# A third chunk normalised among the experts, and an end shared out between three engines, in a one-core mixture-of-experts kernel

## The chip, the cores and the metric

The kernel runs on one core of a Trainium2 chip. The metric is the device time of that core in microseconds (us). Engines: TensorE (PE, and PEld for its weight loads), VectorE (DVE), ScalarE (ACT), GpSimd (POOL), and SyncE (SP), which issues most DMAs. Each takes its instructions in order; semaphores join them.

## The reference, cut to what matters

The input x is 16 batches of 128 rows of 128 numbers, 2048 rows in all. Four blocks are added to it in turn. The change touches the seam inside the first block and the end of the last one.

```python
x = x + L0_attn(L0_cond(x))   # L0_cond: shared expert + two chosen experts of 8 (gelu(g) * u @ down)
                              # L0_attn: layer norm; u, v, base = silu(xn @ W); quadratic attention; @ Wo
x = x + L0_ffn(L0_cond2(x))   # quantised feed-forward, scales from maxima over the whole tensor
x = x + L1_attn(L1_cond(x))
x = x + L1_ffn(L1_cond2(x))   # L1_ffn, the last:
    w = router weights (rows x 16)
    q, k, v = einsum('ne,neh->nh', w, x @ proj[e])      # for each of three projections
    o = softmax(q k^T / sqrt(128)) v
    out = einsum('enh,ehc->nc', w[:, e] * o, o_proj)    # 16 experts e
```

## The kernel before, in words

The rows stand in four chunks `c` of 512 rows (columns of the transposed tiles), each of four tiles `b` of 128. A product that needs more than half precision is written as three f16 matmuls (high by high, and the two mixed ones: `PASSES`, `SPLIT`); an f32 matmul of 128x128 shows as two records.

**The experts of the first block.** The list `order` (L226 to L235) fixes the order of the units on TensorE, ScalarE and VectorE by hand: 16 shared units, then four groups of eight expert units ("ex"). A unit is `up` on TensorE into a pair of PSUM banks (`pair(k)`, three pairs in turn), gelu on ScalarE (L905), the gating product on VectorE (L1366), a half-precision copy on ScalarE (L915), its rest on VectorE (L1372), and three places later `down` on TensorE. Between the units stand steps of the layer norm of chunks already finished: "mean" (L450, then `centred`, L1303, and ScalarE's square), "var" (L455, `variance`), and "rs": ScalarE writes the inverse root as a diagonal (`diag`, L884, four activations of 128x128), TensorE spreads it (`rstd`, L464), VectorE scales (`xg`, L1337), ScalarE and VectorE split the result in two halves (`xn_hi` L893, `xn_lo` L1341). The inverse root itself is a chain of small VectorE instructions on 128xn numbers (`inverse_root`, L1311 to L1332), each waiting for the one before.

In the kernel before, chunks 0 and 1 are wholly normalised among the experts of group 3. Chunk 2 has mean and variance there. Chunk 3 has nothing, since its rows are ready only with the last unit (L1397). What is left stands behind the experts: TensorE L479 to L521, ScalarE L928 to L951, VectorE L1406 to L1423. There are three projections `base`, `u0`, `u1` of each chunk (L496), each followed by a silu on ScalarE (L935); chunk c uses bank BK[4 + c] for all three, so each waits for the silu before it. After them come a small product for the third block (`ret_amm`, copied by ScalarE at L951), eight steps of `v` (L538, L542, silu L961), VectorE's quantisation of feed-forward weights (`prep_fw`, L1251), 32 rotations (L1436) whose inputs GpSimd prepares (L1858), and `fw_lo` (L1428), which waits for ScalarE's copies of the turned weights (L973). VectorE's next work (L1445 on) comes behind `fw_lo`.

**The end.** For chunks 0 to 2, `output(n)` on TensorE multiplies a tile of attention output by four experts' matrices (three f16 matmuls of 128x512, L809) into one of three banks. VectorE's `gather(n)` (L1751) adds the four blocks into the tile of XT, each times its column of router weights: four dependent instructions. There are 48 such groups, four for each tile, and `RW` (the weights) is multiplied by the softmax's inverse sums beforehand (L1799). The third bank turn of `output` waits for a gather three groups back.

Chunk 3 goes another way. When its attention output is in BK[4] (`attend(3, 2)`, L796, which waits for ScalarE's `ptt(3)`, L1103), VectorE weighs it for each of the 16 experts (`ZW[e1]`, L1817), and TensorE multiplies each by the expert's matrix in f32, 128x128 for each tile (`weighed_output`, L841), summing in four banks. Experts 12 to 15 are done tile by tile, and each tile is finished by one instruction of VectorE (L1825). The gathers of the last four groups of chunk 2, 44 to 47 (they are tile 11), stand between the weighings. SyncE sends each tile of 64 KB out as it is finished (L1993), in the order of the tiles.

Of the kernel before, what the change touches and what calls it, by code (L numbers as in the profile page):

```python
# [13 lines left out]
ALU = mybir.AluOpType  # L14
# [37 lines left out]
    (("down", 48), ("weffmm", 4), ("ret_amm", 1), ("fwt", 3), ("wbotmm", 8), ("zmm", 4), ("mlp_down", 16), ("prod_o", 48), ("tile", 4)),  # L52
# [12 lines left out]
     ("ff_max", 24), ("gate16", 4), ("gated_ff", 5), ("ot_ff", 4), ("o_lo", 12), ("x2", 4), ("pp", 4), ("w2", 2), ("weighed", 64), ("zw", 16)),  # L65
# [4 lines left out]
    (("x_lo", 4), ("xq", 4), ("quant", 12), ("ot_lo", 3)),  # L70
    (("route", 30), ("router", 114), ("rw", 3), ("done", 4)),
# [41 lines left out]
def program(nc, A, out):  # L113
    with ExitStack() as ctx:
# [112 lines left out]
        for g in range(4):  # L227
            ex = [("ex", 4 * g + bi, s) for bi in range(4) for s in range(2)]
            if g:
                ex[6:6] = [("var", g - 1, 0)]  # L230
                ex[4:4] = [("mean", g - 1, 0)]
            if g == 3:
                ex[3:3] = [("rs", 1, 0)]
                ex[2:2] = [("rs", 0, 0)]
            order += ex  # L235
# [27 lines left out]
        ROOT = 12  # L263
# [23 lines left out]
        BK_M = [BK[i] for i in (7, 2, 3, 1, 0, 1, 0, 1)]  # L287
        PROJ = {"base": (512, "bb", BASE), "u0": (0, "bu0", U0), "u1": (128, "bu1", U1)}
# [86 lines left out]
        ZW += [STG[:, i // 3, 512 * (i % 3):512 * (i % 3) + 512] for i in range(6)] + [PK0T[:, 512 * i:512 * i + 512] for i in range(2)]  # L375
        SPREADS = 4
# [8 lines left out]
        def tensor(e):  # L385
# [101 lines left out]
            def project(name, c):  # L487
# [4 lines left out]
                else:  # L492
                    q.wait_ge({"u0": "base", "u1": "u0"}[name], c + 1)
                w = PROJ[name][0]
                for n, (wp, xp) in enumerate(SPLIT):
                    t = e.matmul(BK[4 + c][:, :], AW16[:, wp, w:w + 128], XH[:, xp, cc(c)], start=(n == 0), stop=(n == 2))  # L496
                t.then_inc(S(name + "mm"), 1)

            q.wait_ge("gated", UNITS)
            weff(0)  # L500
# [4 lines left out]
            project("base", 1)  # L505
            weff(2)
            weff(3)
            project("u0", 0)
            project("u0", 1)
            q.wait_ge("cent", 4)  # L510
            rstd(2, BK[0])
            q.wait_ge("var", 4)
            rstd(3, BK[1])
            for c in range(2):
                project("u1", c)
            for name in ("base", "u0", "u1"):
                for c in (2, 3):
                    project(name, c)
# [4 lines left out]
            def turn_ffn(i):  # L523
                q.wait_ge("prep", PREP["fq"])
                q.wait_ge("u1", i + 1)
# [310 lines left out]
            def weighed_output(e1, b):  # L836
# [4 lines left out]
                return e.matmul(BK_T[b][:, 0:128], ZW[e1][:, bb_(b)], WO[:, bb_(e1)], start=(e1 == 0), stop=(e1 == 15), skip_group_check=True)  # L841
# [11 lines left out]
        def scalar(e):  # L853
# [30 lines left out]
            def diag(c):  # L884
                q.wait_ge("root", ROOT if c < 2 else 2 * ROOT)
# [9 lines left out]
            for k in range(NU + 3):  # L895
                if k + 1 < NU and order[k + 1][0] == "rs":
                    diag(order[k + 1][1])
                if k < NU and order[k - 1][0] == "rs":
# [33 lines left out]
            def project(name, c):  # L932
                _, b, dst = PROJ[name]
                q.wait_ge(name + "mm", c + 1)
                e.activation(dst[:, cc(c)], BK[4 + c][:, :], ACT.Silu, bias=col(b), scale=1.0 / AS).then_inc(S(name), 1)  # L935

            project("base", 0)
            project("base", 1)
            diag(2)
            diag(3)  # L940
            project("u0", 0)
            xn_hi(2)
            project("u0", 1)
            xn_hi(3)
            for c in range(2):
                project("u1", c)
            for name in ("base", "u0", "u1"):
                for c in (2, 3):
                    project(name, c)
# [155 lines left out]
            for k in range(STEPS):  # L1105
# [22 lines left out]
                if k >= LAG and k < NI + LAG and (k - LAG) % 16 == 15:  # L1128
# [4 lines left out]
                    e.activation(VS[:, cc(c)], BK[2][:, :], ACT.Copy).then_inc(S("qv_out"), 1)  # L1133
            softmax(3)
            ptt(3)

        def vector(e):
# [167 lines left out]
            def variance(c, bank):  # L1305
                q.wait_ge("varmm", c + 1)
                if c == 2:
                    e.tensor_copy(sm(15), bank[:, 16:32]).then_inc(S("sim_sq"), 1)
# [776 lines left out]
```

## Time and profile before

| what | us |
|---|---|
| median of 3 runs | 487.17 (486.77 to 487.62) |
| profiled execution, its own time | 487.26 |
| its span, first to last instruction | 485.5 |
| TensorE busy | 435.0 (90%) |
| VectorE busy | 411.2 (85%) |
| ScalarE busy | 244.7 (50%) |
| GpSimd busy | 63.3 (13%) |

The span runs from the first to the last instruction; 1.76 us of the profiled execution lie around it. All times below are counted from the span's start. Busy shares are averages over stages with different limits. In the timelines each row is an instruction or a run of equal ones: start, duration, engine, line, operation, output and inputs with shapes, and in brackets how long the engine had been idle before it and for whom. Durations of one engine overlap a little, so the step from one start to the next is shorter than a duration.

### The profile page before, as it was taken

How to read it: one execution, taken by the hardware profiler on the slowest of the kernel's cores; microseconds unless marked ns; L12 is line 12 of the kernel's file. 1: busy time of each engine (PE TensorE's matmuls, PEld its weight loads, DVE VectorE, ACT ScalarE, POOL GpSimd, SP SyncE). 2: the span in 40 equal slices, each digit the busy share in tenths (PEclk: the TensorE clock that was granted, in tenths of full speed). 3: DMA queues.
4: the chain of work that ended last, by engine and by line, in shares of the span. 5: the costliest groups of instructions: out<-in, count | busy, mean ns of one | idle time of the engine just before them, and what ended most of it. 6: DMA issues, size and time to landing. Idle time of an engine off the chain costs nothing.

```text
span 485.5 us, 9701 instructions
## 1 busy us (share of the span) xinstructions
PE 435.0 (90%) x3783; PEld 302.5 (62%) x3783; DVE 411.2 (85%) x919; ACT 244.7 (50%) x446; POOL 63.3 (13%) x77
## 2 busy tenths in 40 slices
PE   8999999998898989202999999999999999999997
PEld 6447998987357654000389867667666555655576
DVE  6997889786698769999866789986998999989786
ACT  5976554474767549893666463336224222422110
POOL 0007000000690706300090000000000000000000
PEclk9999999999999999755899999999999999999999
DMA  8979996960560005303330025637753000000000
GB/s 274 355 304 395 388 383 280 372 269 10 166 174 1 1 0 159 101 14 124 122 99 1 1 76 189 212 139 248 259 195 97 7 12 7 5 7 7 5 7 28
DMA packets 24629, 66.71 MB, mean 137 GB/s; under 512 B 3108, under 2 KB 6567, under 8 KB 24455
## 3 DMA queue, kind: packets, MB, share of 16 engines
q1 hardware_dynamic: 24144, 65.98, 37.7%
q8 instruction: 30, 0.49, 0.4%
q10 hardware_dynamic: 438, 0.11, 0.1%
q14 instruction: 17, 0.13, 0.1%
HBM read 38.68 MB, written 1.18 MB: 82 GB/s over the span
## 4 chain that ended last, share of the span: by engine, by line
PE 29%; DVE 22%; issue 4%; ACT 1%; DVEq 0%; ACTq 0%
PE bk L764 10%; DVE XT L1751 6%; PE bk L772 5%; DVE X L1739 3%; PE bk L809 3%; DVE RA L1779 3%; PE bk L631 2%; DVE RA L1558 1%; DVE WK L1600 1%; PE bk L784 1%; PE bk L674 1%; PE bk L640 1%; PE bk L691 1%; DVE QS L1466 1%; PE bk L700 1%
## 5 line engine op out<-in xcount | busy, mean ns | idle before, releaser
L764 PE MATMUL bk<-X,RB 128*128 128x512 f16 x384 | 94.6, 383 | 0.7 <-DVE X L1739 0.4
L1069 ACT ACTIVATE X<-RA 128x512 f16<-128x512 f32 x64 | 40.3, 630 | 101.2 <-DVE RA L1779 83.9
L1751 DVE SCALAR_TENSOR_TENSOR XT<-bk,WK,XT 128x128 f32<-128x128 f32 x192 | 67.0, 349 | 5.4 <-issue 0.2
L764 PEld LDWEIGHTS bk<-X,RB 128*128 128x128 f16 x384 | 37.1, 99 | 42.3 <-DVE X L1739 1.6
L772 PEld LDWEIGHTS bk<-RB,X 128*128 128x128 f16 x768 | 48.8, 99 | 15.4 <-issue 0.6
L772 PE MATMUL bk<-RB,X 128*128 128x128 f16 x768 | 53.8, 220 | 0.0
L1739 DVE TENSOR_TENSOR X<-RA,X 128x512 f16<-128x512 f32 x64 | 43.9, 685 | 1.3 <-ACT X L1069 1.3
L905 ACT ACTIVATE WK<-bk 128x512 f32<-128x512 f32 x48 | 28.6, 595 | 27.5 <-PE bk L418 21.7
L809 PE MATMUL bk<-RB,RA 128*128 128x512 f16 x144 | 38.8, 379 | 0.9 <-DVE RA L1796 0.9
L1366 DVE SCALAR_TENSOR_TENSOR RB<-WK,WCOL,bk 128x512 f32<-128x512 f32 x32 | 23.7, 744 | 10.1 <-ACT WK L905 10.1
L418 PE MATMUL bk<-X,RC 128*128 128x128 f16 x480 | 29.7, 219 | 0.0
L1372 DVE TENSOR_TENSOR RB<-RB 128x512 f16<-128x512 f32 x36 | 25.6, 712 | 3.9 <-ACT RB L915 3.6
L418 PEld LDWEIGHTS bk<-X,RC 128*128 128x128 f16 x480 | 27.9, 98 | 0.9
L915 ACT ACTIVATE RB<-RB 128x512 f16<-128x512 f32 x36 | 22.4, 624 | 5.8 <-DVE RB L1366 5.6
L413 PE MATMUL bk<-X,STG 128*128 128x512 f16 x96 | 22.8, 379 | 0.2 <-DVE X L1179 0.2
L1466 DVE TENSOR_REDUCE QS<-RA 128x1 f32<-128x512 f32 (+2 forms) x28 | 22.4, 837 | 0.1
L594 PE MATMUL bk<-PK1T,QS 128*128 128x128 f32 x5 | 2.1, 413 | 20.5 <-DVE QS L1469 20.5
L1858 POOL TENSOR_SCALAR RA<-RA,ROPE 128x128 f32<-128x128 f32 x16 | 9.4, 590 | 81.4 <-ACT RA L935 81.4
L413 PEld LDWEIGHTS bk<-X,STG 128*128 128x128 f16 x96 | 9.3, 97 | 15.5 <-issue 6.0
L447 PE MATMUL bk<-RB,RC 128*128 128x128 f16 x240 | 16.6, 219 | 2.6 <-DVE RB L1372 2.6
L809 PEld LDWEIGHTS bk<-RB,RA 128*128 128x128 f16 x144 | 12.7, 98 | 7.3 <-DVE RA L1796 1.3
L447 PEld LDWEIGHTS bk<-RB,RC 128*128 128x128 f16 x240 | 14.2, 98 | 4.7 <-DVE RB L1372 2.9
(345 smaller groups left out, 884.9 us busy)
## 6 DMA issues: line engine op xcount, KB each, us to landing
RC<-RA SPq DMA_DIRECT2D x20, 768.0 KB, 5.2
STG<-RA SPq DMA_DIRECT2D x8, 768.0 KB, 5.4
RC<-expert_weights SPq DMA_DIRECT2D x22, 256.0 KB, 6.0
RC<-in_wx SPq DMA_DIRECT2D x7, 768.0 KB, 7.8
X<-in_w SPq DMA_DIRECT2D x8, 512.0 KB, 3.5
RA<-RA SPq DMA_DIRECT2D x4, 768.0 KB, 5.1
STG<-expert_weights SPq DMA_DIRECT2D x12, 256.0 KB, 5.9
QT<-expert_weights SPq DMA_DIRECT2D x8, 256.0 KB, 5.0
```

What stands on the lines that cost most here:

```text
L413: t = e.matmul(bank[:, :], W16[:, o:o + 128], X16[:, xp, cc(a)], start=(n == 0), stop=(n == 2))
L418: t = e.matmul(bank[:, bb_(jj)], w[:, o:o + 128], X16[:, xp, bb_(a)], start=(n == 0), stop=(n == 2))
L447: t = e.matmul(bank[:, bb_(a % 4)], w[:, o:o + 128], H16[:, u % 3, xp, bb_(jj)], start=(j == 0 and jj == 0 and n == 0), stop=(j == 1 and j ...
L764: t = e.matmul(BK[m][:, :], P16[:, wp, wo:wo + 128], ZH[:, n % 4, xp, :], start=(e1 == 0 and i == 0), stop=(e1 == 15 and i == 2))
L772: t = e.matmul(BK[2][:, bb_(b)], ZH[:, n % 4, xp, bb_(b)], P16[:, wp, wo:wo + 128], start=(e1 == 0 and b == 0 and i == 0), stop=(e1 == 15 ...
L809: t = e.matmul(bank_o(n)[:, :], OT16[:, xp, bb_(4 * c + b)], P16[:, wp, 6144 + 512 * g:6656 + 512 * g], start=(i == 0), stop=(i == 2))
L905: e.activation(ge[u % 3], pair(k)[0][:, :], ACT.Gelu_apprx_tanh, scale=1.0 / WS).then_inc(S("gelu"), 1)
L1069: e.activation(ZH[:, r, 0, :], zf[r], ACT.Copy).then_inc(S("z_hi"), 1)
L1372: tt(H16[:, u % 3, 1, :], hf[u % 3], H16[:, u % 3, 0, :], ALU.subtract).then_inc(S("h_lo"), 1)
L1466: return red(dst, src, X_AX, ALU.max, apply_absolute_value=True)
L1739: tt(ZH[:, n % 4, 1, :], zf[n % 4], ZH[:, n % 4, 0, :], ALU.subtract).then_inc(S("zlo"), 1)
L1751: stt(XT[:, bb_(t_)], bank_o(n)[:, bb_(i)], RW[:, t_, e1:e1 + 1], XT[:, bb_(t_)], ALU.mult, ALU.add).then_inc(S("acc"), 1)
```

## The change

1. `order` of group 3 holds mean 2 one place earlier and a new last place, "rs" of chunk 2. The root of chunk 2 is a chain of its own, ten steps, spread over the places behind "var" 2. `ROOT` is 10: the clamp below is dropped for the layer norm and moved into another instruction for the router's columns, and the clamp above is done once for those columns alone, behind the last chain.
2. Behind the experts only chunk 3 is normalised. The projections run over chunks 0, 1, 2 first and chunk 3 last; in chunk 3 `u0` uses bank 6 instead of 7. `prep_fw(0)` is moved up, before `xg(3)`.
3. At the end the gathers of groups 44 to 47 leave VectorE. ScalarE (`late`) multiplies the four blocks of each by their weights into SBUF, and GpSimd adds the sixteen blocks together (six additions) and to the tile.
4. Chunk 3 is weighed before the product for experts 0 to 11 (`PRE` = 12). Experts 12 to 15 are weighed behind it: TensorE does four more `output` groups, 48 to 51, and VectorE four more gathers. This needs the attention output of chunk 3 in halves (two instructions of VectorE from BK[4]) and `RW` of chunk 3 times its inverse sums (one small one).

```diff
+                ex = ex[0:2] + [("rs", 0, 0), ex[2], ("rs", 1, 0), ("mean", 2, 0)] + ex[3:5] + [("var", 2, 0)] + ex[5:8] + [("rs", 2, 0)]
-        ROOT = 12
+        ROOT = 10
+        def bank_p(name, c):
+            return BK[6 if c == 3 and name == "u0" else 4 + c]
+        PRE, LATE = 12, 44
+        groups += [(3, b, 3) for b in range(4)]
+        WGT = [XF[:, 512 * i:512 * i + 512] for i in range(4)]
@@ TensorE behind the experts @@
             q.wait_ge("gated", UNITS)
+            q.wait_ge("xg", 3)
...
             project("base", 1)
+            project("base", 2)
             weff(2)
             weff(3)
-            project("u0", 0)
-            project("u0", 1)
-            q.wait_ge("cent", 4)
-            rstd(2, BK[0])
+            for c in range(3):
+                project("u0", c)
             q.wait_ge("var", 4)
             rstd(3, BK[1])
-            for c in range(2):
+            for c in range(3):
                 project("u1", c)
             for name in ("base", "u0", "u1"):
-                for c in (2, 3):
-                    project(name, c)
+                project(name, 3)
@@ project(u0, 3) waits for u1 of chunk 2, project(u1, 3) for base of chunk 3 @@
@@ output(n) @@
-                q.wait_ge(*(("acc", 4 * (n - 2)) if n >= 3 else ("wts", 3)))
+                if n < 3:
+                    q.wait_ge("wts", 3)
+                elif LATE <= n - 3 < LATE + 4:
+                    q.wait_ge("late_w", n - 2 - LATE)
+                else:
+                    q.wait_ge("acc", 4 * (n - 2 if n - 3 < LATE else n - 6))
...
-            for e1 in range(12):
+            for e1 in range(PRE - 2):
                 for b in range(4):
                     weighed_output(e1, b)
-                if e1 in (0, 4):
-                    output(46 + (e1 == 4))
+                if e1 in (0, 1, 3, 5, 7, 9):
+                    output({0: 46, 1: 47, 3: 48, 5: 49, 7: 50, 9: 51}[e1])
             for b in range(4):
-                for e1 in range(12, 16):
+                for e1 in range(PRE - 2, PRE):
                     t = weighed_output(e1, b)
@@ ScalarE behind the experts @@
-            project("base", 0)
-            project("base", 1)
-            diag(2)
+            for c in range(3):
+                project("base", c)
             diag(3)
-            project("u0", 0)
-            xn_hi(2)
-            project("u0", 1)
+            for c in range(2):
+                project("u0", c)
             xn_hi(3)
-            for c in range(2):
+            project("u0", 2)
+            for c in range(3):
                 project("u1", c)
             for name in ("base", "u0", "u1"):
-                for c in (2, 3):
-                    project(name, c)
+                project(name, 3)
@@ ScalarE at the end @@
+            def late(n):
+                q.wait_ge("prod_o", n + 1)
+                for i in range(4):
+                    e1 = 4 * g + i
+                    t = e.activation(WGT[n - LATE][:, bb_(i)], bank_o(n)[:, bb_(i)], ACT.Copy, scale=RW[:, t_, e1:e1 + 1])
             softmax(3)
+            late(44)
             ptt(3)
+            for n in range(45, 48):
+                late(n)
@@ VectorE behind the experts @@
-            for _ in inverse_root(8, 32):
+            for _ in inverse_root(12, 32):
                 pass
+            then(root)
+            ts(SNS, SNS, 1e12, None, ALU.min)
             weff(2)
-            xg(2, BK[0])
+            prep_fw(0)
             xg(3, BK[1])
+            xn_lo(3)
             weff(3)
-            xn_lo(2)
-            xn_lo(3)
@@ VectorE at the end @@
-            for e1 in range(16):
+            tt(RW[:, 12:16, :], RW[:, 12:16, :], RS[:, 12:16] (broadcast), ALU.mult)
+            for e1 in range(PRE):
                 tt(ZW[e1], BK[4][:, :], WR[16 + e1], ALU.mult)
-                if e1 in (1, 4, 7, 10):
-                    gather({1: 44, 4: 45, 7: 46, 10: 47}[e1])
+                if e1 == 2:
+                    e.tensor_copy(OT16[:, 0, cc(3)], BK[4][:, :])
+                    tt(OT16[:, 1, cc(3)], BK[4][:, :], OT16[:, 0, cc(3)], ALU.subtract)
+                if e1 in (6, 8, 10, 11):
+                    gather({6: 48, 8: 49, 10: 50, 11: 51}[e1])
@@ GpSimd at the end: SUM = WGT[0]; plus WGT[1], WGT[2], WGT[3] (128x512 each), then its halves @@
@@ (128x256, 128x128), then XT of tile 11 plus SUM (128x128), "summed"; tile 11 is sent on "summed" @@
```

## Rows read from the trace of the kernel before

**Rows 1.** The page: busy time, share and instructions by engine.
```profile
PE 435.0 (90%) x3783; PEld 302.5 (62%) x3783; DVE 411.2 (85%) x919; ACT 244.7 (50%) x446; POOL 63.3 (13%) x77
```

**Rows 2.** The chain that ended last, in order of time, 452 us on: start, us.
```profile
462.61 0.65 PE bk L809 x3
463.25 0.04 issue
463.29 1.17 PE bk L796 x8
...
464.49 1.29 DVE RA L1817 x2
...
483.07 0.35 DVE XT L1825
```

**Rows 3.** Timeline of VectorE behind the experts.
```profile
119.75 0.69 DVE L1397 SCALAR_TENSOR_TENSOR QT<-bk,QT 128x512 f32<-128x512 f32 x1 [0.94 <-PE bk L447]
...
124.35 0.18 DVE L1314 TENSOR_SCALAR SM<-SM 128x24 f32<-128x24 f32 x1
124.56 0.18 DVE L1317 TENSOR_SCALAR SM<-SM 128x24 int32<-128x24 int32 x1
...
129.51 0.75 DVE L1337 SCALAR_TENSOR_TENSOR QT<-QT,COL,bk 128x512 f32<-128x512 f32 x1 [2.00 <-PE bk L466]
130.67 0.75 DVE L1337 SCALAR_TENSOR_TENSOR QT<-QT,COL,bk 128x512 f32<-128x512 f32 x1 [0.42 <-PE bk L466]
...
133.38 1.34 DVE L1254 TENSOR_REDUCE QS<-RB 128x36 f32<-128x1152 f32 x1
...
150.76 1.49 DVE L1428 SCALAR_TENSOR_TENSOR FW<-bk,FW 128x384 f16<-128x384 f32 x3 [1.55 <-ACT FW L973]
```

**Rows 4.** Timeline of ScalarE behind the experts.
```profile
126.95 2.44 ACT L888 ACTIVATE WK<-PK1T,SM 128x128 f32<-128x128 f32 x8 [1.27 <-DVE SM L1330]
...
132.10 1.25 ACT L935 ACTIVATE RA<-bk,COL 128x512 f32<-128x512 f32 x2
...
138.08 0.27 ACT L951 ACTIVATE ATT<-bk 128x128 f32<-128x128 f32 x1
```

**Rows 5.** Timeline of TensorE at the last experts and behind them.
```profile
118.09 1.63 PE L447 MATMUL bk<-RB,RC 128*128 128x128 f16 x24 [1.41 <-DVE RB L1372]
...
124.62 1.88 PE L485 MATMUL bk<-WEFF,PK0T 128*128 128x512 f32 x4
126.34 1.46 PE L496 MATMUL bk<-WBOT,AW 128*128 128x512 f16 x6
128.37 2.26 PE L466 MATMUL bk<-WK,ONES 128*128 128x512 f32 x4 [0.57 <-ACT WK L888]
...
132.74 4.72 PE L496 MATMUL bk<-WBOT,AW 128*128 128x512 f16 x18 [0.28 <-DVE WBOT L1341]
137.29 0.38 PE L521 MATMUL bk<-ATT,PK2T 128*128 128x128 f32 x2
138.49 0.37 PE L538 MATMUL bk<-BVD,ON 3*128 3x512 bf16 x1 [0.82 <-ACT ATT L951]
```

**Rows 6.** Timeline of ScalarE: the last softmax, and four activations of PSUM in a row.
```profile
462.01 0.21 ACT L1098 ACTIVATION_READ_ACCUMULATOR WK<-bk,SM 128x1 f32 x1
462.64 0.60 ACT L1103 ACTIVATE RA<-bk 128x512 f32<-128x512 f32 x1 [0.42 <-PE bk L790]
```
```profile
264.13 1.21 ACT L1045 ACTIVATE WK<-bk,BSEL 128x128 f32<-128x128 f32 x4
```

**Rows 7.** Timeline of VectorE at the end.
```profile
465.69 1.50 DVE L1751 SCALAR_TENSOR_TENSOR XT<-bk,WK,XT 128x128 f32<-128x128 f32 x4
467.11 1.28 DVE L1817 TENSOR_TENSOR RA<-bk,WBOT 128x512 f32<-128x512 f32 x2
```

**Rows 8.** Timeline of TensorE at the end: two matmuls of f32 to a row.
```profile
480.19 0.61 PE L841 MATMUL bk<-WEFF,STG 128*128 128x128 f32 x4
480.64 0.61 PE L841 MATMUL bk<-WEFF,PK0T 128*128 128x128 f32 x4
```

**Rows 9.** One line each: durations in ns, min/median/max, first and last start.
```profile
L1404 DVE TENSOR_TENSOR WEFF<-bk,PK0T x4: 679/682/684, 122.3 to 131.3; 128x512 f32<-128x512 f32 x4
```
```profile
L1858 POOL TENSOR_SCALAR RA<-RA,ROPE x16: 447/452/1648, 125.3 to 144.7; 128x128 f32<-128x128 f32 x16
```
```profile
L1835 POOL TENSOR_TENSOR RB<-RB x1: 2810/2810/2810, 37.8 to 37.8; 128x1024 f32<-128x1024 f32 x1
```
```profile
L1993 SPq DMA_DIRECT2D out<-XT x16: 332/332/433, 369.4 to 483.4; - x16
```

More of the change, by code:

```diff
@@ L897, in scalar @@
                     diag(order[k + 1][1])
-                if k < NU and order[k - 1][0] == "rs":
+                if 0 < k <= NU and order[k - 1][0] == "rs":
                     xn_hi(order[k - 1][1])
@@ L1313, in inverse_root @@
                 v, y, h = SMF[:, 224 + a:224 + b], SMF[:, 544 + a:544 + b], SMF[:, 256 + a:256 + b]
-                ts(v, v, 1e-30, None, ALU.max).then_inc(root.next(), 1)
-                yield
-                then(root)
+                if root.n:
+                    then(root)
                 ts(y.bitcast(I32), v.bitcast(I32), -0.5, 1597463007.0, ALU.mult, ALU.add).then_inc(root.next(), 1)
@@ L1328, in inverse_root @@
                     yield
-                then(root)
-                ts(y, y, 1e12, None, ALU.min).then_inc(root.next(), 1)
                 assert root.n % ROOT == 0
-                yield
             def xg(c, bank):
@@ L1388, in vector @@
                     next(first_half, None)
-                if k - 2 < NU and order[k - 2][0] == "rs":
+                if 2 <= k < NU + 2 and order[k - 2][0] == "rs":
                     xn_lo(order[k - 2][1])
@@ L1411, in vector @@
             q.wait_ge("sim_sq", 1)
-            for _ in inverse_root(8, 32):
+            for _ in inverse_root(12, 32):
                 pass
+            then(root)
+            ts(SNS, SNS, 1e12, None, ALU.min).then_inc(root.next(), 1)
             weff(2)
-            xg(2, BK[0])
+            prep_fw(0)
             xg(3, BK[1])
+            xn_lo(3)
             weff(3)
-            xn_lo(2)
-            xn_lo(3)
             then(root)
             tt(SNT, pk1("sim"), SNS, ALU.mult).then_inc(S("sn"), 1)
-            for part in range(4):
+            for part in range(1, 4):
                 prep_fw(part)
@@ L1743, in gather @@
                 t_ = 4 * c + b
+                first = n if n < LATE else n - 4
                 q.wait_ge("prod_o", n + 1)
@@ L1877, in gpsimd @@
                 e.tensor_tensor(lo, src, hi, ALU.subtract).then_inc(S("p16"), 1)
+            SUM = WGT[0]
+            for g in range(1, 4):
+                q.wait_ge("late_w", g + 1)
+                if g > 1:
+                    q.wait_ge("sum", g - 1)
+                e.tensor_tensor(SUM, SUM, WGT[g], ALU.add).then_inc(S("sum"), 1)
+            q.wait_ge("sum", 3)
+            e.tensor_tensor(SUM[:, 0:256], SUM[:, 0:256], SUM[:, 256:512], ALU.add).then_inc(S("sum"), 1)
+            q.wait_ge("sum", 4)
+            e.tensor_tensor(SUM[:, 0:128], SUM[:, 0:128], SUM[:, 128:256], ALU.add).then_inc(S("sum"), 1)
+            q.wait_ge("sum", 5)
+            q.wait_ge("turned", 3)
+            e.tensor_tensor(XT[:, bb_(11)], XT[:, bb_(11)], SUM[:, 0:128], ALU.add).then_inc(S("summed"), 1)
         def sync(e):
@@ L1991, in sync @@
                     t_ = 4 * c + b
-                    q.wait_ge(*(("acc", 4 * groups.index((c, b, 3)) + 4) if c < 3 else ("done", b + 1)))
+                    q.wait_ge(*(("done", b + 1) if c == 3 else ("summed", 1) if t_ == 11 else ("acc", 4 * groups.index((c, b, 3)) + 4)))
                     e.dma_start(out[bb_(t_), :], XT[:, bb_(t_)]).then_inc(S(f"out{c}"), 16)
```

47 lines of the change are left out of this document (29 added, 18 removed).

## The prediction, made before the change was run

> **What bounds the kernel now.** I read the page first: TensorE 90% busy, VectorE 85% [rows 1]. No single engine is the bound, so what matters is which wait ends last at the two places the change touches. The chain that ended last was the second view. It answers for the end of the span, but was followed back only to about 212 us, so for the seam behind the experts (116 to 151 us) I used the timelines of the three engines and read who waits for whom.
>
> At the end the chain goes ScalarE's ptt(3), attend(3, 2) at 463.29, the first weighing at 464.49, then VectorE with hardly a gap (16 weighings, 4 gathers) until the last weighing at 479.8, then TensorE's last tiles and the last L1825 at 483.07 [rows 2]. The reader is to see that VectorE sets the pace to 479.8 and TensorE from there: the last 16 matmuls cannot start before the last weighing.
>
> At the seam there is one chain: last down product, L1397 at 119.75, mean, variance, root from 124.35, eight diagonals from 126.95, two spreadings from 128.37, xg(3) at 130.67 [rows 3, 4, 5]. Then six projections from 132.74 to 137.3, the copy at 138.08, and the v steps from 138.49, which ScalarE and TensorE share until ScalarE frees itself for the turned weights, for which VectorE waits 1.55 us before L1428 at 150.76 [rows 3, 4, 5]. After that VectorE is the next in line (L1445), so a gain at the v steps goes on, as long as VectorE is not itself later by more than it gains: its slack there is those 1.55 us.
>
> **Part 1 and 2, the seam: what is added before it.** Among the last units VectorE gets ten root steps (step 124.35 to 124.56, 0.21 each: 2.1 us), one xg and one xn_lo (about 0.65 each); ScalarE gets four diagonals (2.44 / 8, 0.3 each: 1.2 us) and one xn_hi (0.6); TensorE gets one spreading (half of 2.26 less overlap: 1.0 us) [rows 3 to 5]. TensorE's up products set the pace of the units and stay where they were. Its extra spreading falls into the 1.41 us for which it stood idle before the last two down products [rows 5]: that hides it, and without that gap it would cost its 1.0 us. VectorE's root steps go into waits for gelu between units. The diagonals stand ahead of the last gelu on ScalarE, and xg(2) ahead of the last L1372 on VectorE. Laid out place by place, the last gelu is some 0.25 us later, xg(2) adds 0.65 ahead of the last rest, and some of this was waiting before: the last down product, and L1397, come 0.55 us later. Bounds: 0 (every added step in a gap) and 1.2 (diagonals wholly in front of the gelu). I take 0.55. xn_lo(2) fits while the last down product runs.
>
> **The seam: what is removed behind it.** Times without the 0.55. Root: one step fewer in front and one behind, 0.4 us; four diagonals fewer, 1.2 us. But TensorE's queue now holds more in front of the spreading: base 2 and u0 2 (0.65 each: 1.46 for six matmuls less 0.16 of overlap, halved). The two weff end 1.72 after their start (124.62 to 126.34), now from 125.27, so to 127.0; three u0 to 128.95. The diagonals are ready at 126.5 + 1.2 = 127.7. So the spreading starts at 128.95, 0.58 later than before, bound by TensorE and no more by the root. One spreading instead of two lets xg(3) start 1.14 later (129.51 - 128.37), at 130.1, against 130.67 [rows 3, 4, 5].
>
> Then ScalarE: xn_hi(3) at 130.9 (0.6 to the next), u0 2 to 132.1, so u1 2 on TensorE at 132.15 and base 3 at 132.8, and ScalarE's u1 0, u1 1, u1 2 (0.6 each) to 133.9; u0 3 needs the bank of u1 2, so 133.9 to 134.6; u1 3 needs base 3's silu, so 134.6 to 135.25. Its silu is issued at 135.45 and the copy L951 at 136.05, the first v step at 136.4. Before: 138.49. That is 2.1 us, and with the 0.55 added before it 1.55 us net [rows 4, 5]. The size comes from nine matmuls left behind xn_lo(3) where there were eighteen (4.72 us), less the waits that one chunk alone cannot cover.
>
> VectorE keeps up: after xg(3) and xn_lo(3) it has weff(3) and the last three parts of prep_fw. Part 0, the reduction of 1.34 at 133.38 and two small ones, 2.0 us, now lies in the wait before xg(3) (2.00 us idle there [rows 3]); two thirds of it would be lost with that wait. It finishes the rotations 1.7 us earlier, more than 1.55. GpSimd gets chunk 2's base some 7 us earlier, and at 0.45 each [rows 9] it stays ahead of the rotations. So -1.55 us goes through; bounds -2.1 (0 before) and -0.9 (1.2 before).
>
> **Part 3, tile 11.** VectorE loses four gathers of 1.42 us (465.69 to 467.11) and part 4 gives it four others [rows 7]. ScalarE's late(44) stands ahead of ptt(3): four activations from PSUM, 1.21 for such a four or a step of 0.29, from 462.1, so ptt(3) starts at 463.25 instead of 462.64 [rows 6]. Behind it are attend(3, 2) and every weighing: +0.6 us, bounds +0.4 and +0.8. The other three lates lie beside VectorE. GpSimd's additions: 2.81 us for 1024 columns [rows 9], 2048 columns in all, so an estimate of 5.6 us, from about 470.5 on for the last 2.9; tile 11 is out by 475, well ahead of the first tile of chunk 3. Cost nothing; the cover is some 5 us.
>
> **Part 4, the end.** VectorE from 465.1: seven weighings of 0.60 (1.28 less 0.68) [rows 7], the copy and the rest (0.69 each, one wait between, 1.35): 470.65. It then wants group 48. TensorE begins at 465.8: four experts of 16 f32 matmuls in all at 0.2225 (0.445 for two [rows 8]) are 3.56, three outputs at 0.65 [rows 2] are 1.95: 471.3. VectorE waits to 471.4. Four gathers and five weighings: 5.68 + 3.0, to 480.1. TensorE's first part (40 matmuls, 8.9, six outputs, 3.9) ends at 478.6, so it is never more than 1.6 us ahead of need. The last weighing is done at 478.7; eight matmuls end at 480.6, beside the last gather. VectorE's four last instructions (0.27 apart) then end at 481.2, against 483.42. SyncE takes 0.33 to 0.43 us to issue one [rows 9], more than 0.27, so the fourth goes at 480.5 + 3 x 0.4 = 481.65 against 483.45. Net -1.8 us with the +0.6 in it; bounds -2.4 and -0.9 (slowest issues, every output waited for).
>
> **Rule and row: GpSimd beside VectorE.** While GpSimd worked without a break from 125.3, VectorE's L1404, one input in PSUM and one in SBUF like the weighings, took 679 to 684 ns, as the weighings do without GpSimd (1.28 for two) [rows 7, 9]. So I add nothing. GpSimd's own instructions were at times stretched from 447 to 1648 ns [rows 9]. In a sentence of its own: the Trainium skill, page "Perfetto Trace Analysis", section "Optimizing Scalar/DVE Operations", warns that the two share an SBUF read port, so offloading between them might not help; by that rule alone the additions would hold VectorE up. Its page "SBUF — State Buffer", section "Who interferes with whom", narrows this to VectorE instructions with two SBUF inputs or in a two-port mode; by that, the sum stands as it is, and the L1404 row agrees.
>
> **Sum.** -1.55 - 1.8 = -3.35 us on the profiled execution of 487.26, whose span is 485.5: 483.9. The median, 487.17, is 0.09 below that execution, so 483.8; I say 483.9.
>
> **Rivals.**
> - *Both gains, as summed*: 483.9; its own range 482.9 to 484.9. Chance 0.60.
> - *The end gives more, or the units hide all*: -2.1 and -2.4: 482.7. For it: long waits for gelu among the units. Against: TensorE has little room at the end. 0.10.
> - *The seam gives nothing*: diagonals and root steps delay the units by 2.1 us, or the u chain of chunk 3 runs at ScalarE's pace. For it: the in-order queues, the spreading now behind three u0. 487.2 - 1.8 = 485.4. 0.13.
> - *The end gives nothing*: TensorE becomes the bound, each gather waits for its output, issues are slow. 487.2 - 1.55 = 485.6. 0.08.
> - *The change does nothing to the time*: both of these. 487.2. 0.05.
> - *Slower: GpSimd's additions hold VectorE.* Place: 466 to 475, price up to 5.6 us [rows 9]: 483.9 + 5.6 = 489.5. It decides against the change from 3.4 us of blocking on. Against: L1404. 0.04.
>
> 0.2% is 1 us, about what a measurement here can tell from no change. Faster than 486.2: the first four, 0.91, less 0.02 for the high ends of the two middle ones, 0.89; same 0.05 + 0.02; slower 0.04. The range that leaves out 2 in 10: 482.5 to 485.7.
>
> **What would show it.** Right: L1397 about 0.5 us later, at 120.3; the spreading not waiting for the diagonals; nine L496 matmuls behind xn_lo(3); the first v step at about 137; ptt(3) near 463.3 less the 1.55; VectorE waiting for output(48) once, under 1 us; the last four L1825 back to back, the end of the span near 482.1. Wrong: gelu waits of over 1 us for the diagonals; weighings of over 0.7 us beside GpSimd; TensorE idle before groups 49 to 51; the fourth tile's DMA far behind the last L1825; or a stage in between that holds the gain back by waiting for a transfer.

## The result, and the profile after

| | before | after |
|---|---|---|
| median (6 runs each, us) | 487.39 (486.62 to 488.02) | 484.91 (484.23 to 485.41) |
| profiled execution, its own time | 487.26 | 484.23 |
| its span | 485.5 | 482.3 |

The ratio is 0.9941, with a 95% interval of 0.9916 to 0.9966: 0.6% faster. A second set of six runs gave the same 0.9941 (0.9928 to 0.9954). Against 487.17 that ratio is a gain of 2.9 us, where the forecast was 3.3; the two medians of the table lie 2.5 apart, those of the second set 2.9. 483.9 was forecast, and 482.5 to 485.7 as the range; the median came out at 484.91. Both parts gained, the case that had been called likeliest.

Some executions of the changed kernels took 4 to 5 us longer than the rest, at a mean granted TensorE clock of 0.954 or 0.955 instead of 0.958 to 0.968; the last section is on them.

To see where the time went both traces are cut at the same nine events and the stretches compared. That is better than comparing start times, since a gain shifts everything behind it. In the table each event is the start of an instruction: "diagonals" is ScalarE's first diagonal of group 3, "residual" the last instruction that adds a down product (L1397 before, L1421 after), "first v" TensorE's first v step, "fw_lo" the first L1428 before and L1453 after, "router work" VectorE's first L1779 before and L1805 after, "attend" the last matmul of attend(3, 0), "weighing" the first L1817 before and L1845 after. Only "done" is an end, that of the last L1825 or L1856. seam_only and end_only are the first two experiments.

| stretch, us | before | after | seam_only | end_only |
|---|---|---|---|---|
| diagonals to residual | 21.22 | 21.85 | 21.84 | 21.22 |
| residual to xg(3) | 10.92 | 10.24 | 10.24 | 10.92 |
| xg(3) to first v | 7.82 | 6.37 | 6.37 | 7.86 |
| first v to fw_lo | 12.27 | 12.27 | 12.27 | 12.27 |
| fw_lo to the first router work of the third block | 135.52 | 135.34 | 135.61 | 135.33 |
| from there to attend | 173.19 | 172.83 | 173.15 | 172.78 |
| attend to weighing | 5.02 | 5.51 | 5.01 | 5.51 |
| weighing to done | 18.93 | 16.40 | 18.93 | 16.40 |
| done to the end of the span | 2.04 | 2.69 | 2.04 | 2.69 |

The first four rows are the seam: 52.2 against 50.7, a gain of 1.5. The last three are the end: 26.0 against 24.6, a gain of 1.4. The rest of the 3.2 between the spans (0.3 more ahead of the first row, 0.5 less in the two middle ones) is no part of the change: two_queues, a later experiment that does all of it up to the end as the changed kernel does, has 135.54 and 173.18 in the middle rows, like the kernel before.

**The seam.** VectorE's timeline of the kernel after, which answers to [rows 3]:

```profile
119.89 0.75 DVE L1362 SCALAR_TENSOR_TENSOR WBOT<-QT,COL,WBOT 128x512 f16<-128x512 f32 x1 [0.19 <-ACT WBOT L904]
120.64 0.69 DVE L1421 SCALAR_TENSOR_TENSOR QT<-bk,QT 128x512 f32<-128x512 f32 x1
...
130.89 0.75 DVE L1358 SCALAR_TENSOR_TENSOR QT<-QT,COL,bk 128x512 f32<-128x512 f32 x1 [0.77 <-PE bk L473]
...
149.53 1.49 DVE L1453 SCALAR_TENSOR_TENSOR FW<-bk,FW 128x384 f16<-128x384 f32 x3 [1.92 <-ACT FW L982]
```

The last residual, L1421, carries no bracket: VectorE did not wait for the down product in front of it but came to it straight from xn_lo(2) (L1362). Before, VectorE waited 2.00 us in front of xg(2) and 0.42 in front of xg(3). Now one wait of 0.77 is left, in front of xg(3), since part 0 of prep_fw stands there. The wait in front of fw_lo grew from 1.55 to 1.92, so VectorE did not hold the gain back.

TensorE's and ScalarE's timelines of the kernel after, which answer to [rows 4, 5]:

```profile
119.76 0.84 PE L454 MATMUL bk<-RB,RC 128*128 128x128 f16 x12 [0.42 <-DVE RB L1396]
...
127.88 2.11 PE L503 MATMUL bk<-WBOT,AW 128*128 128x512 f16 x9
129.83 1.02 PE L473 MATMUL bk<-WK,ONES 128*128 128x512 f32 x2
130.68 1.46 PE L503 MATMUL bk<-WBOT,AW 128*128 128x512 f16 x6
133.02 1.47 PE L503 MATMUL bk<-WBOT,AW 128*128 128x512 f16 x6 [0.88 <-ACT RA L946]
134.75 1.47 PE L503 MATMUL bk<-WBOT,AW 128*128 128x512 f16 x6 [0.26 <-ACT RA L946]
```

```profile
127.38 1.28 ACT L899 ACTIVATE WK<-PK1T,SM 128x128 f32<-128x128 f32 x4 [0.23 <-DVE SM L1351]
...
131.67 0.72 ACT L904 ACTIVATE WBOT<-QT,COL 128x512 f16<-128x512 f32 x1 [1.60 <-DVE QT L1358]
132.29 2.98 ACT L946 ACTIVATE RA<-bk,COL 128x512 f32<-128x512 f32 x5
135.61 1.33 ACT L946 ACTIVATE RA<-bk,COL 128x512 f32<-128x512 f32 x2 [0.34 <-PE bk L503]
136.84 0.27 ACT L960 ACTIVATE ATT<-bk 128x128 f32<-128x128 f32 x1
```

Three things are to be seen. The spreading of chunk 3 (L473 at 129.83) does not wait for its diagonals, which end at 128.66; it starts when the nine L503 in front of it are done. Behind xn_hi(3) ScalarE works on five silus without a pause, and TensorE waits for it twice, 0.88 and 0.26 us. And the copy L960 stands at 136.84.

**The end.** The chain of work that ended last, of the kernel after, answers to [rows 2] (start, us, instruction):

```profile
463.95 1.16 PE bk L852 x8
...
476.37 0.66 PE bk L820 x3
477.06 0.36 DVE XT L1777
```

This view names TensorE from the first weighing to the last output, 463.95 to 477.03. VectorE's timeline, and two rows of TensorE's, say more:

```profile
463.20 0.69 DVE L1845 TENSOR_TENSOR RA<-bk,PK0T 128x512 f32<-128x512 f32 x1 [0.93 <-PE bk L802]
...
469.76 1.51 DVE L1777 SCALAR_TENSOR_TENSOR XT<-bk,WK,XT 128x128 f32<-128x128 f32 x4 [0.96 <-PE bk L820]
...
472.39 1.50 DVE L1777 SCALAR_TENSOR_TENSOR XT<-bk,WK,XT 128x128 f32<-128x128 f32 x4
...
475.00 1.50 DVE L1777 SCALAR_TENSOR_TENSOR XT<-bk,WK,XT 128x128 f32<-128x128 f32 x4
...
477.06 1.51 DVE L1777 SCALAR_TENSOR_TENSOR XT<-bk,WK,XT 128x128 f32<-128x128 f32 x4
478.48 1.12 DVE L1856 SCALAR_TENSOR_TENSOR XT<-bk,SM,XT 128x128 f32<-128x128 f32 x4
```

```profile
471.99 1.95 PE L852 MATMUL bk<-WEFF,QT 128*128 128x128 f32 x16
...
474.43 1.95 PE L852 MATMUL bk<-WEFF,STG 128*128 128x128 f32 x16
```

VectorE waits once, 0.96 us for output(48), and is then busy to the end. TensorE was done with output(49) and output(50), and went on to the next experts, at 471.99 and 474.43; VectorE took them at 472.39 and 475.00. Only output(51) came together with VectorE: the weighing in front of it starts at 476.42, a step of 0.60 later is 477.02, and the gather starts at 477.06. So TensorE sets the time up to 469.76 and VectorE from there on, and the chain names TensorE for that last tie. GpSimd's and SyncE's timelines show the rest of the new end:

```profile
463.06 1.27 POOL L1916 TENSOR_TENSOR X<-X 128x512 f32<-128x512 f32 x1 [208.98 <-ACT X L1153]
...
471.23 0.46 POOL L1923 TENSOR_TENSOR XT<-XT,X 128x128 f32<-128x128 f32 x1
```

```profile
478.86 1.75 SPq L2039 DMA_DIRECT2D out<-XT  x4
```

GpSimd's additions are six, five for the sixteen blocks and one into the tile. They take 5.44 us in all and are over by 471.7, ten microseconds before the span ends. SyncE issues the last four tiles one behind the other, 1.75 us for four, while VectorE finished them in 1.12. The last issue ends at 480.61, and the span 1.7 us later. Before, the last issue ended at 483.78, also 1.7 us ahead of the end, but only 0.4 behind VectorE's last instruction instead of 1.0.

### The profile page after: what moved, and what is told of

Same layout as the page of the kernel before. It is cut to its first block, busy times and chain, and to the rows that moved or that the text cites. A ratio compares the mean times of both kernels' runs of the same rounds, so it can differ in the third digit from the quotient of the medians.

```text
span 482.3 us, 9698 instructions
## 1 busy us (share of the span) xinstructions
PE 430.7 (89%) x3763; PEld 299.2 (62%) x3763; DVE 410.9 (85%) x925; ACT 248.5 (52%) x462; POOL 68.8 (14%) x83
## 4 chain that ended last, share of the span: by engine, by line
PE 27%; DVE 23%; issue 4%; ACT 2%; DVEq 0%
PE bk L770 8%; DVE XT L1777 5%; DVE X L1764 4%; PE bk L778 4%; PE bk L820 4%; DVE RA L1805 4%; PE bk L852 2%; PE bk L637 2%; DVE RA L1583 1%; DVE WK L1625 1%; PE bk L790 1%; PE bk L646 1%; PE bk L680 1%; PE bk L697 1%; DVE QS L1491 1%
## 5 line engine op out<-in xcount | busy, mean ns | idle before, releaser
L820 PE MATMUL bk<-RB,RA 128*128 128x512 f16 x156 | 42.0, 379 | 0.9 <-DVE RA L1822 0.9
L916 ACT ACTIVATE WK<-bk 128x512 f32<-128x512 f32 x48 | 28.5, 594 | 27.0 <-PE bk L425 21.4
L1916 POOL TENSOR_TENSOR X<-X 128x512 f32<-128x512 f32 x3 | 3.8, 1269 | 211.9 <-ACT X L1153 211.9
L1396 DVE TENSOR_TENSOR RB<-RB 128x512 f16<-128x512 f32 x36 | 25.7, 714 | 2.6 <-ACT RB L926 2.4
L820 PEld LDWEIGHTS bk<-RB,RA 128*128 128x128 f16 x156 | 13.8, 98 | 7.9 <-DVE RA L1822 1.3
```

The lines of the kernel that those rows point to most:

```text
L820: t = e.matmul(bank_o(n)[:, :], OT16[:, xp, bb_(4 * c + b)], P16[:, wp, 6144 + 512 * g:6656 + 512 * g], start=(i == 0), stop=(i == 2))
L916: e.activation(ge[u % 3], pair(k)[0][:, :], ACT.Gelu_apprx_tanh, scale=1.0 / WS).then_inc(S("gelu"), 1)
L1396: tt(H16[:, u % 3, 1, :], hf[u % 3], H16[:, u % 3, 0, :], ALU.subtract).then_inc(S("h_lo"), 1)
```

## The experiments

All edits are to the changed kernel unless said otherwise, and none leaves out part of the computation except gpsimd_more, which adds five additions on numbers that nobody reads.

**1 and 2. The two parts alone.** seam_only has the changed experts and seam with the end of before; end_only has the old seam with the changed end (`PRE`, `LATE`, groups 48 to 51, ScalarE's `late`, GpSimd's additions).

> Only the seam's part of the change; the end stays as before. Theory (the forecast's steps): the last L1397 comes 0.5 to 0.7 us later than before, the first v step 1.2 to 1.6 us earlier, and all of it goes through, so the time is about 1.5 us below before (ratio 0.997) and the stretch from attend(3, 0) to the end is as before, 24.6 us. Rival (the seam gives nothing, all the gain is the end's): ratio 1.000 and the first v step within 0.3 us of before. Rival (the two parts lean on each other): this plus the end's part alone does not add up to the whole change.

> Only the end's part of the change; the seam stays as before. Theory: from attend(3, 0) to VectorE's last instruction 22.5 us instead of 24.6, and 0.6 us more from there to the end of the span because four transfers are issued one behind another, so the time is about 1.4 us below before (ratio 0.997) and everything up to attend(3, 0) is as before within the scatter of the clock. Rival (the end gives nothing on its own): ratio 1.000.

seam_only: 485.7 us (485.14 to 486.25), ratio 0.9966 (0.9953 to 0.9978): 1.66 us. end_only: over twelve runs the ratio is 1.0002 (0.9978 to 1.0027). Three of the twelve had clock 0.955 and took 490.1 to 490.8; the median of the other nine is 485.93, 1.3 us below before. In the table above each part shows its own stretches and leaves the other's alone, to 0.1 us. So the parts add up: 1.5 and 1.4 make 2.9, as measured for the whole. The timed ratio of end_only alone can't show the gain; its trace does.

**3. The changed kernel again.**

> The whole change, run beside its two parts on one chip. If the parts are independent, its gain is the sum of the two: about 2.9 us, ratio 0.994. If they lean on each other it differs from the sum by more than 1 us.

484.35 us (483.96 to 488.9), ratio 0.9941 (0.9928 to 0.9954). All stretches agree with the first trace to 0.1 us but one: from the third block's router work to attend it took 177.5 instead of 172.8, which is 4.7 us more. That is the profiled execution at clock 0.954. TensorE's busy time and granted clock (PEclk, the column behind POOL) by windows, of this trace:

```profile
core 0: us, PE busy (x) PEld busy (x) DVE busy (x) ACT busy (x) POOL busy (x), PEclk, DMA share, GB/s
286.00:290.00 4.00, 4.00 (x16) 1.70 (x16) 3.83 (x14) 2.75 (x8) 0.00 (x0) 0.61 0.91 259
290.00:294.00 4.00, 4.00 (x25) 3.62 (x23) 3.79 (x13) 1.35 (x4) 0.00 (x0) 0.50 0.91 258
294.00:298.00 4.00, 4.00 (x16) 2.35 (x16) 3.65 (x11) 0.26 (x1) 0.00 (x0) 0.50 0.72 273
298.00:302.00 4.00, 4.00 (x32) 2.60 (x30) 1.53 (x4) 0.64 (x2) 0.00 (x0) 0.68 0.00 1
302.00:306.00 4.00, 4.00 (x39) 2.63 (x38) 3.02 (x10) 1.25 (x2) 0.00 (x0) 1.00 0.00 0
```

and of the first trace of the same kernel:

```profile
286.00:290.00 4.00, 4.00 (x16) 1.82 (x15) 3.83 (x13) 2.75 (x8) 0.00 (x0) 0.57 0.85 260
290.00:294.00 4.00, 4.00 (x37) 3.17 (x36) 3.79 (x13) 1.34 (x4) 0.00 (x0) 1.00 1.03 355
```

The kernel is the same, and so is the work, but TensorE's clock falls to half (1.2 GHz) for 13.7 us in the one and 3.4 us in the other, added up from the rows.

**4. GpSimd beside VectorE.** gpsimd_more puts five more additions of 128x512 behind the last one, so that GpSimd works beside VectorE through the end:

```diff
+            for i in range(5):
+                if i:
+                    q.wait_ge("more", i)
+                e.tensor_tensor(WGT[1], WGT[1], WGT[2], ALU.add).then_inc(S("more"), 1)
```

> GpSimd is given five more additions of 128x512 (their sums are used by nothing) right behind its last one, so that it works beside VectorE's weighings and gathers until about 478 us. If a weighing with one input in PSUM and one in SBUF does not contend with GpSimd: its duration stays 0.68 us, the step 0.60, a gather's four 1.50, and the end is where it was. Rival (GpSimd's additions hold VectorE up): each addition of 1.27 us costs a weighing or gather up to its own length, and the last VectorE instruction comes 1 to 6 us later.

A timeline and the groups of lines of this kernel (in the second, mean ns stands behind busy us):

```profile
471.50 6.66 POOL L1927 TENSOR_TENSOR X<-X 128x512 f32<-128x512 f32 x5
```

```profile
L1777 DVE SCALAR_TENSOR_TENSOR XT<-bk,WK,XT 128x128 f32<-128x128 f32 x16 | 5.6, 350 | 1.4 <-PE bk L820 1.0
L1845 DVE TENSOR_TENSOR STG<-bk,RC 128x512 f32<-128x512 f32 x4 | 2.6, 680 | 0.0
```

The weighings took 680 ns beside a busy GpSimd, 681 in the changed kernel, 680 in the one before. The gathers took 350, and all stretches of the end stayed (5.5, 16.4, 2.7). The rival in which GpSimd holds VectorE is refuted. The rows agree with the Trainium skill, page "SBUF — State Buffer", section "Who interferes with whom", by which an instruction of VectorE with at most one SBUF input, outside its two-port modes, does not contend with GpSimd. The warning of the Trainium skill, page "Perfetto Trace Analysis", section "Optimizing Scalar/DVE Operations", did not come true here.

**5. What late(44) costs in front of ptt(3).** late_behind:

```diff
-            late(44)
             ptt(3)
+            late(44)
```

> ScalarE does ptt(3) first and late(44) behind it. Theory (late(44) delays the way to the first weighing): from attend(3, 0) to the first weighing 0.5 to 0.6 us less than in the changed kernel (6.12), as before (5.64), and the last VectorE instruction 0.5 us earlier, since output(47), which waits for late(44), comes 3 us later than that. Rival (the delay was covered by something else): the first weighing does not move.

attend to weighing took 5.0 us instead of 5.5, as before the change, and the rest of the end stayed within 0.1. ScalarE's two instructions in its timeline:

```profile
465.35 0.60 ACT L1112 ACTIVATE RA<-bk 128x512 f32<-128x512 f32 x1 [0.42 <-PE bk L796]
465.84 2.17 ACT L1153 ACTIVATE X<-bk,WK 128x128 f32<-128x128 f32 x8
```

ptt(3) (L1112) waits for its matmuls, no longer for ScalarE. The term is 0.5 us (forecast 0.6). The single time of this kernel, 488.07, was again one at clock 0.954, and says nothing about the edit.

**6. The seam behind xg(3).** u0_before_hi gives ScalarE the silu of `u0` 2 before it splits chunk 3:

```diff
-            xn_hi(3)
             project("u0", 2)
+            xn_hi(3)
```

> ScalarE does the silu of u0 chunk 2 before xn_hi(3), in the 1.60 us for which it waits for xg(3) in the changed kernel, instead of behind it. Theory (from xn_hi(3) to the v steps ScalarE's queue of silus is the bound): the copy L960 and the first v step come 0.6 us earlier. Rival (TensorE's matmuls behind xn_lo(3) are the bound): they move by less than 0.2 us.

xg(3) to first v took 5.8 us instead of 6.4. In ScalarE's timeline a silu has moved from behind the wait to in front of it (three and four, where there were two and five):

```profile
128.78 1.98 ACT L946 ACTIVATE RA<-bk,COL 128x512 f32<-128x512 f32 x3
131.71 0.72 ACT L904 ACTIVATE WBOT<-QT,COL 128x512 f16<-128x512 f32 x1 [0.95 <-DVE QT L1358]
132.34 2.51 ACT L946 ACTIVATE RA<-bk,COL 128x512 f32<-128x512 f32 x4
```

So behind xg(3) ScalarE's queue of silus is the bound, and one silu less in it is 0.5 us less to the v steps (0.54 before rounding).

**7 and 8. What makes the last residual 0.6 us later.** rest_first moves xg(2) on VectorE behind the rest (the subtraction L1396) of its place, so that the last down products get their input earlier:

```diff
-                        xg(a, BK[2 * (k % 3)])
+                        if a < 2:
+                            xg(a, BK[2 * (k % 3)])
...
+                if k < NU and order[k] == ("rs", 2, 0):
+                    xg(2, BK[2 * (k % 3)])
```

> VectorE takes the rest of the last unit (L1396) ahead of xg(2) instead of behind it. Theory (xg(2), 0.66 us, stands in front of the last down product): the last down product and L1421 come 0.4 to 0.6 us earlier, and the v steps with them. Rival (the late gelu behind the four diagonals is all of the delay, xg(2) lies in a wait): L1421 moves by less than 0.15 us.

This was a miss. Diagonals to residual came to 22.55 us, 0.7 more than in the changed kernel (21.85), and not less. TensorE's and VectorE's timelines of rest_first say why:

```profile
117.28 2.47 PE L454 MATMUL bk<-RB,RC 128*128 128x128 f16 x36
119.66 1.10 PE L492 MATMUL bk<-WEFF,PK0T 128*128 128x512 f32 x2
```

```profile
120.30 0.75 DVE L1362 SCALAR_TENSOR_TENSOR WBOT<-QT,COL,WBOT 128x512 f16<-128x512 f32 x1 [0.79 <-ACT WBOT L904]
120.97 0.68 DVE L1424 SCALAR_TENSOR_TENSOR QT<-bk,QT 128x512 f32<-128x512 f32 x1
```

The last down products did come earlier: TensorE ran them without a wait and went on to weff at 119.66 (120.44 in the changed kernel). But xg(2) was later, so ScalarE's half of the split was later, and VectorE stood 0.79 us in front of xn_lo(2), with the residual queued behind it although its product was there. both_behind therefore moves xn_lo(2) as well, from its old place to behind the residual (shown here is only where it goes):

```diff
+                        if g == 3:
+                            xn_lo(2)
```

> As rest_first, and xn_lo(2) is taken behind L1421 and the addition that follows it. Rest_first brought the last down product forward by 0.8 us, but L1421 then waited for xn_lo(2), and that for ScalarE's xn_hi(2). Theory (those two stand in front of the last sum): from the first diagonals to L1421 21.3 to 21.5 us, against 21.8 in the changed kernel and 22.6 in rest_first, and xg(3) and the first v step come earlier by nearly as much. Rival (the mean of chunk 3 is then held up by xn_lo(2), so that nothing is left): xg(3) where the changed kernel has it.

Diagonals to residual: 21.4 us (21.37), 0.5 less than in the changed kernel and 0.15 more than in the kernel before (21.22); span 481.6, time 483.49. VectorE's timeline, with the residual now in front and waiting for its product alone:

```profile
119.84 0.69 DVE L1424 SCALAR_TENSOR_TENSOR QT<-bk,QT 128x512 f32<-128x512 f32 x1 [0.28 <-PE bk L454]
...
121.18 0.74 DVE L1362 SCALAR_TENSOR_TENSOR WBOT<-QT,COL,WBOT 128x512 f16<-128x512 f32 x1
```

So two things together cost 0.5 of the 0.6 us: xg(2) in front of the last rest, and xn_lo(2) in front of the residual. In the changed kernel they end together (the down product at 120.60, xn_lo(2) at 120.64), which is why moving the one alone brought nothing.

The other 0.15 is still there in both_behind, and ScalarE's timelines show where it comes from. First the last gelu of the changed kernel with the diagonals in front of it, then that of the kernel before:

```profile
115.32 1.26 ACT L899 ACTIVATE WK<-PK1T,SM 128x128 f32<-128x128 f32 x4
116.49 0.58 ACT L916 ACTIVATE WK<-bk 128x512 f32<-128x512 f32 x1
```

```profile
116.05 0.60 ACT L905 ACTIVATE WK<-bk 128x512 f32<-128x512 f32 x1 [1.41 <-PE bk L418]
```

Counted from the first diagonal of group 3 (98.80 and 98.53), the last gelu starts at 17.69 in the changed kernel and at 17.52 in the one before. In both_behind it is 17.69 too. So chunk 2's diagonals fill the 1.41 us for which ScalarE waited before, and hold up the last gelu by 0.17.

**9 and 10. TensorE's outputs one expert earlier.** outputs_early lets output(48) and those behind it start one expert sooner:

```diff
-                if e1 in (0, 1, 3, 5, 7, 9):
-                    output({0: 46, 1: 47, 3: 48, 5: 49, 7: 50, 9: 51}[e1])
+                if e1 in (0, 1, 2, 4, 6, 8):
+                    output({0: 46, 1: 47, 2: 48, 4: 49, 6: 50, 8: 51}[e1])
```

> TensorE takes output groups 48 to 51 behind experts 2, 4, 6 and 8 instead of 3, 5, 7 and 9. Theory (the end is TensorE's pace up to output(51), on which VectorE's last gather waits): the wait for output(48), 0.96 us, shrinks to under 0.2, the last gather starts 0.6 to 0.8 us earlier, and then TensorE's eight last matmuls are the bound, so VectorE's last instruction comes 0.4 to 0.7 us earlier. Rival (VectorE is the bound anyway): under 0.2 us.

> The kernel of outputs_early once more. In its one look VectorE's last instruction came 0.5 us earlier, counted from the first weighing, but the span ended 3.85 us behind that instruction instead of 2.65. If the late end was one transfer landing late by chance: 2.6 to 2.8 this time, and the 0.5 us are kept. If it belongs to the order: 3.8 again.

Weighing to done was 16.0 us in both traces, against 16.4: 0.4 less. The wait for output(48) is gone (from the first trace; no bracket):

```profile
469.06 1.51 DVE L1777 SCALAR_TENSOR_TENSOR XT<-bk,WK,XT 128x128 f32<-128x128 f32 x4
```

0.96 us of waiting gave only half of itself back, since VectorE's last four instructions now wait for TensorE (1.60 us for the four where it was 1.12). Done to the end of the span was 3.8 us in the first trace and 2.2 in the second, of one and the same program. In the first the last tile landed 2.8 us behind the end of its issue; in the second, and in every other trace here, it was 1.2. So the 3.8 is one slow transfer and no part of the order; why it was slow stays open. The 2.2 is 0.5 less than the 2.7 of the changed kernel: the last four tiles are now finished over 1.60 us, hardly faster than SyncE issues them (1.75), so the issues no longer pile up.

**11. The last tiles from two queues.** two_queues has ScalarE send tiles 13 and 15 and SyncE 12 and 14:

```diff
+            for b in (1, 3):
+                q.wait_ge("done", b + 1)
+                e.dma_start(out[bb_(12 + b), :], XT[:, bb_(12 + b)]).then_inc(S("out_act"), 16)
```

> ScalarE's queue issues the transfers of tiles 13 and 15, SyncE those of 12 and 14. Theory (four issues of 0.33 to 0.43 us, one behind another on SyncE, stretch the end): from VectorE's last instruction to the end of the span 2.0 to 2.3 us, as before, instead of 2.65 to 2.75. Rival (the four transfers share the 16 DMA engines and land late for that): it stays at 2.6.

Done to the end of the span: 2.1 us instead of 2.7, nearly the 2.0 of the kernel before. The timeline of all engines:

```profile
478.96 0.85 SPq L2044 DMA_DIRECT2D out<-XT  x2
479.23 0.87 ACTq L1163 DMA_DIRECT2D out<-XT  x2
```

**12. All five edits together** (late(44) behind ptt(3), u0 2 before xn_hi(3), xg(2) and xn_lo(2) behind, outputs earlier, two queues).

> The changed kernel with everything that the single runs suggest: ScalarE's ptt(3) ahead of late(44), its u0 of chunk 2 ahead of xn_hi(3), VectorE's last rest ahead of xg(2) and xn_lo(2) behind L1421, output groups 48 to 51 an expert earlier, the last transfers on two queues. If the gains add: 0.5 + 0.4 at the seam, 0.5 + 0.5 + 0.5 at the end, some 2.4 us below the changed kernel, ratio to before 0.989. Rival (they meet, since the same engine is next in line at both places): under 1.2 us below the changed kernel.

Median 481.98 us (481.09 to 486.43, the highest at clock 0.954), ratio to before 0.9917 (0.9888 to 0.9946). It beats both kernels, and is 2.4 us below the changed kernel's 484.35. Its stretches are 21.4, 10.3, 5.8, 12.3 at the seam and 5.0, 16.0, 2.1 at the end. Against the changed kernel that is 0.9 less at the seam and 1.5 less at the end. At the seam it is the sum of what each edit gave alone (0.4 and 0.5). At the end it is the 0.5 of late(44), the 0.4 of the earlier outputs up to VectorE's last instruction, and 0.6 behind it. For that last 0.6 two edits compete: by the second trace of experiment 10 the earlier outputs alone give 0.5 of it, the two queues alone all of it, and together they gave 0.6 and not 1.1.

## Why the prediction was right, and where it was off

- **The seam's size, -1.55 forecast, -1.5 measured.** The parts came out too. From the diagonals to the residual 0.55 was to be added, and 0.6 was. xg(3) was to start 0.02 us earlier than before (130.65 against 130.67); counted from the diagonals it started 0.05 earlier. The first v step was to be at 136.95 and was at 137.26, of which 0.3 lies ahead of the diagonals.
- **What delays the residual.** The forecast made its 0.55 from a gelu 0.25 later and an xg(2) of 0.65, part of it covered. The gelu is 0.17 later, and 0.15 of it reaches the residual; moving xg(2) and xn_lo(2) together gave back 0.47. The step "xn_lo(2) fits while the last down product runs" was right only as a tie: it ends 0.04 us behind the down product. By that, taking xg(2) alone out of the way gains nothing, which rest_first's expectation missed.
- **The spreading bound by TensorE's queue and not by the root**: right, by 1.2 us (129.83 against 128.66).
- **ScalarE's silus as the bound behind it**: right, and u0_before_hi showed what one silu there is worth, 0.5 us.
- **GpSimd costs nothing**: right. 5.44 us of additions against an estimate of 5.6; more than doubling them moved nothing. The row of L1404 was thinner support than the text made it: GpSimd's work begins at 125.3, and two of the four L1404 lie before that, at 122.27 and the step after it.
- **late(44)**: 0.6 forecast, 0.5 measured, shown by taking it out of the way.
- **The end's size, -1.8 forecast, -1.4 measured: the term that was mis-sized.** From weighing to done the forecast had -2.8 (481.2 against 483.42, the 0.6 taken out), and the trace shows -2.5. The difference lies in front of output(48), in TensorE. From the first weighing to the end of VectorE's wait 6.3 us were forecast (465.1 to 471.4) and 6.56 measured (463.20 to 469.76). Of these 0.26, TensorE's start behind the weighing has 0.05, its work up to the end of output(48) 0.1 (5.61, to 469.56, against 5.5), and the hand-over to VectorE 0.1 (0.20 against 0.1). Behind the wait 9.8 were forecast and 9.84 measured, with VectorE leading again, as the forecast said. From done to the end of the span it had 0.4 more, from issues of 0.4 us against finishes of 0.27, and it is 0.65 more; four issues took 1.75 us, 0.44 each.
- **Not priced at all: TensorE's clock in the third block.** It has no visible part in the medians of the changed kernel, but it adds to the scatter of whole executions, and it is why the end's gain can't be read from end_only's ratio.

## What to carry to other kernels

When work is moved into gaps of other engines, write down for each in-order queue what stands behind the moved instruction. An instruction that waits for its input holds what is ready behind it, as xn_lo(2) did in rest_first, and where two causes end within 0.04 us of each other only moving both shows a gain. When the last instructions of a kernel come closer together, the issue of their output transfers becomes a term of its own: here 0.6 us, given back by a second queue, or for the most part by spreading the last instructions out again. The chain that ended last names one engine where two arrive together, so read the waits of both before saying which one leads. And cut the traces at the same events before weighing a gain of under 1%: the stretches of the change repeated to 0.1 us where two profiled executions of one program differed by 4.7.

## What the runs showed of the hardware that had not been expected

In most of the profiles TensorE's granted clock falls to half (1.2 GHz) twice before the end. The first time it lasts from some 200 to 230 us, when TensorE is nearly idle. The second begins between 286 and 290 us, behind a stage (266 to 286 us) in which TensorE was 79 to 100% busy in windows of 4 us, with no gap over 0.44 us, and had the full clock. The last work before the second fall in the profile of after is small: matmuls of 16 columns and of one column (L716 and L719, 284.69 to 286.4). The first window at full clock began at 294 us in the profile of before, at 290 in the first of after and at 302 in that of after_again, and in the profile of all_mends there was no second fall. Window rows of before, then of all_mends:

```profile
286.00:290.00 4.00, 3.56 (x27) 2.67 (x26) 3.83 (x14) 1.79 (x5) 0.00 (x0) 0.94 0.49 141
290.00:294.00 4.00, 4.00 (x27) 2.62 (x25) 3.80 (x13) 2.43 (x6) 0.00 (x0) 0.64 1.01 295
```

```profile
286.00:290.00 4.00, 3.57 (x32) 2.68 (x32) 3.79 (x12) 2.95 (x8) 0.00 (x0) 1.00 0.92 298
```

The long one costs 4.7 us (177.5 against 172.8 for the stretch). Executions with a mean clock of 0.954 or 0.955 came once in twelve runs of the changed kernel, three times in twelve of end_only and once in six of all_mends, and in none of the 35 runs of before, the longest of which took 488.36. The one profile of late_behind had it too, again for 13.7 us. All six lie in kernels with the changed end (38 runs in all), none in those with the old end (40 runs, the five of seam_only among them), although the fall comes some 170 us ahead of the first instruction in which the two ends differ. end_only does what before does up to 458 us, so the changed seam is not needed for it. Whether that is chance, and what decides how long the clock stays low, was not tried and stays open. The first fall has two lengths as well, 31 and 34 us; with it go the two middle rows of the table, 135.3 to 135.4 and 172.8 where it is 31 us (after, end_only, both_behind, all_mends), 135.5 to 135.6 and 173.0 to 173.2 where it is 34 (before, seam_only and the rest, but for the two profiles with the long second fall). The Trainium skill, page "TensorE: Matmul & The Clock Gate", section "Part 1: The HAM clock gate (the "warmup" mystery)", tells of a clock that falls when TensorE is idle. The first fall agrees with that. The second does not come behind idleness as far as these rows show it, and there the measurement decides; its cause stays open.
